# Float32r projections in layers 0, 2 and 3, weight magnitudes on ACT, and a moved residual and norm in a four-layer megakernel

## The reference, cut to what matters

```python
x = x + _L0_xattn_ref(_layernorm(x), ctx_1024, mask, ...)   # 16 heads of 16, softmax over 4096 keys
x = x + _L0_attn_ref(_layernorm(x), ...)
x = x + _L0_ffn_ref(_layernorm(x), L0_ffn_w1, ...)
x = x + _L1_xattn_ref(...); x = x + _L1_attn_ref(...); x = x + _L1_ffn_ref(...)   # 16 experts, top 2
x = x + _L2_xattn_ref(ctx_1024, _layernorm(x)); x = x + _L2_attn_ref(...); x = x + _L2_ffn_ref(...)
x = x + _L3_xattn_ref(_layernorm(x), ctx_1024, ctx_1024, ...); x = x + _L3_attn_ref(...)
x = x + _L3_ffn_ref(...)                                      # two layers inside
# layer 0, attention: h is the normed x with scale and bias
c_q = h @ w_down_q.T;  c_kv = h @ w_down_kv.T
q = c_q @ w_up_q.T;  k = c_kv @ w_up_k.T;  v = c_kv @ w_up_v.T    # 128 -> 1024 each, then rotary on q and k
# layer 0, feed-forward: weights are rounded to -1, 0, 1
scale = 1.0 / jnp.clip(jnp.mean(jnp.abs(w)), 1e-05)
wq = jnp.clip(jnp.round(w * scale), -1, 1) / scale
# layer 2, attention: t is the rms-normed x; q, k, v are 1024 wide, a gate per head
q = t @ Wq;  k, v = split(t @ Wkv)
# layer 2, feed-forward
out = sigmoid(xr @ W_r.T) * (square(relu(xk @ W_k.T)) @ W_v.T)
# layer 3, cross attention: of each head's 16 keys the top KEEP = 11 stay; linear attention
# layer 3, feed-forward, each of two layers: attention of 8 heads, then
a, g = split(layernorm(x) @ w1 + b1);  x = x + (a * gelu(g)) @ w2 + b2
```

## Time and profile before

| what | value |
|---|---|
| median of 3 runs | 2007.03 us (2000.08 to 2008.4) |
| the profiled execution's own time | 2001.91 us |
| its span | 2000.6 us |
| PE, DVE, ACT, POOL busy | 95%, 68%, 62%, 35% of the span |
| mean granted TensorE clock | 0.989 |
| instructions | 38492 |

### The profile page before, as it was taken

How to read it: one execution, slowest core, us unless ns; L and a number is a source line. 1 busy time by engine, 2 the same in 40 slices (tenths; PEclk the granted TensorE clock), 3 DMA queues, 4 the chain that set the end, 5 groups by cost and what they waited for, 6 DMA issues and landing times.

```text
span 2000.6 us, 38492 instructions
## 1 busy us (share of the span) xinstructions
PE 1894.7 (95%) x14304; PEld 1204.0 (60%) x14329; DVE 1354.4 (68%) x3178; ACT 1248.9 (62%) x2811; POOL 706.3 (35%) x899
## 2 busy tenths in 40 slices
PE   7999999989999899999999999999999899899999
PEld 4555665545465645566555556879657688565656
DVE  3677668765486677766879577774356998578382
ACT  3687778867363458777888673367265786265251
POOL 2123331173460211333110155676042566355151
PEclk9999999987999999999999999999999999999999
DMA  9677668753011497766876113164102342200110
GB/s 214 145 147 150 120 120 164 127 92 106 1 43 53 77 149 148 152 118 122 164 128 93 37 52 98 49 204 123 48 22 77 93 120 61 90 1 9 43 57 11
DMA packets 114362, 191.58 MB, mean 96 GB/s; under 512 B 17224, under 2 KB 67201, under 8 KB 107649
## 3 DMA queue, kind: packets, MB, share of 16 engines
q1 hardware_dynamic: 113184, 188.11, 42.9%
q10 hardware_dynamic: 992, 1.02, 0.2%
HBM read 135.20 MB, written 2.69 MB: 69 GB/s over the span
## 4 chain that ended last, share of the span: by engine, by line
PE 66%; DVE 21%; ACT 7%; issue 2%; POOL 2%; DMA 1%; SPq 0%; POOLq 0%; ACTq 0%; DVEq 0%
DVE WK L900 10%; PE PS L837 8%; PE PS L708 8%; PE PS L738 6%; PE PS L381 5%; PE PS L389 4%; PE PS L696 4%; ACT WK L586 3%; PE PS L2499 2%; PE PS L539 2%; PE PS L2441 2%; PE PS L491 2%; PE PS L518 2%; PE PS L754 2%; PE PS L1369 1%
## 5 line engine op out<-in xcount | busy, mean ns | idle before, releaser
L900 DVE TENSOR_REDUCE WK<-PS 128x1 f32<-128x1024 f32 x512 | 621.1, 1223 | 218.4 <-PE PS L708 170.3
L1008 ACT ACTIVATE WK<-PS 128x512 f32<-128x512 f32 x840 | 464.9, 601 | 45.0 <-PE PS L708 30.8
L708 PEld LDWEIGHTS PS<-QSR,KSR 51*128 51x128 f32 x2048 | 253.3, 189 | 242.0 <-ACT WK L1008 92.0
L708 PE MATMUL PS<-QSR,KSR 51*128 51x256 f32 x2048 | 381.4, 309 | 8.9 <-DVE WK L900 0.9
L696 PE MATMUL PS<-KSR,QSR 51*128 51x512 f32 x1024 | 371.6, 452 | 3.6 <-DMA KSR<-scratch_mask 2.8
L837 PE MATMUL PS<-WK 128*32 128x256 f32 x2528 | 223.4, 400 | 0.5 <-ACT WK L992 0.5
L614 POOL TENSOR_SCALAR WK<-WK 128x256 f32<-128x256 f32 (+1 forms) x320 | 150.9, 472 | 164.3 <-ACT WK L586 62.9
L1023 POOL TENSOR_TENSOR WK<-WK 128x512 fp32r<-128x512 f32 x62 | 79.2, 1278 | 350.9 <-ACT WK L969 177.0
L696 PEld LDWEIGHTS PS<-KSR,QSR 51*128 51x128 f32 x1024 | 187.2, 187 | 13.2 <-DVE WK L900 6.5
L586 ACT ACTIVATE WK<-PS,WK 128x256 f32<-128x256 f32 (+1 forms) x320 | 140.4, 450 | 62.3 <-DVE WK L558 42.0
L1126 POOL TENSOR_SCALAR nbw<-WK 128x4 fp32r<-128x4 f32 x64 | 12.6, 197 | 314.2 <-DVE WK L906 313.3
(11 more groups left out here) (388 smaller groups left out, 3897.9 us busy)
## 6 DMA issues: line engine op xcount, KB each, us to landing
KSR<-WK SPq DMA_DIRECT2D x381, 128.0 KB
WB<-in_ctxT SPq DMA_DIRECT2D x78, 512.0 KB, 5.1
WK<-in_ctxT SPq DMA_DIRECT2D x40, 512.0 KB, 4.1
WK<-in_ctx SPq DMA_DIRECT2D x32, 512.0 KB, 3.9
WA<-in_ctxT SPq DMA_DIRECT2D x26, 512.0 KB, 5.1
QSR<-scratch_q SPq DMA_DIRECT2D x48, 128.0 KB, 4.4
WB<-in_L3f_qkv SPq DMA_DIRECT2D x2, 1536.0 KB, 6.3
WB<-in_L3f_w SPq DMA_DIRECT2D x2, 1536.0 KB, 10.2
```

Source lines behind the costliest of these rows:

```text
L708: return pe.e.matmul(tile["S", L, s, i][:, j * 256:j * 256 + 256], KS[s % 4][HALF[i % 2], kt * 128:(kt + 1) * 128], QS[HALF[i % 2], g % 2, ...
L900: dv.e.tensor_reduce(mt[:, n:n + 1], tile["R", L, s, n].rearrange("p a b -> p (a b)"), AX, ALU.max).then_inc(*dv.at("R", L, s, n))
L1008: ac.e.activation(PR[n % NPR], tile["S", L, s, i], ACT.Exp).then_inc(*ac.at("E", L, s, i))
```

## The change

It has five parts.

1. *Cross attention 0.* POOL's `magnitude` and `total` go. ACT computes Abs of each half weight with a sum over its columns, after the Exp of score tiles 5 and 13 of step 26 and 5 and 9 of step 27 (`ABS`), and TensorE adds the halves. `last` is issued at the start of step 25. POOL splits the four up-projection weights into a high part in `CXR` and a low part in `WBR` (`split_up`) in its last three turns. One normalisation of the first head group (`normalise`) is done some row maxima later.
2. *Layer 0's attention.* The query and key tiles are three float32r matmuls each; `c0` is split by DVE and ACT.
3. *Layer 2's attention.* The first two query tiles stay float32; keys, values and the other six query tiles are float32r, in this order. High parts are made by ACT, low parts of weights by POOL, of activations by DVE.
4. *Layer 2's feed-forward and cross attention 3.* DVE's tail keeps its product; POOL adds the residual in one instruction, DVE takes the norm's statistics over units 4 to 7, ACT the inverse root by Ln and Exp, POOL normalises at 8, TensorE transposes at 9. Unit 0 moves from the sixth place to the eleventh. `fill` counts change.
5. *Layer 3's feed-forward.* Of each layer's twelve `w1` tiles, eight are float32r.

```diff
+        def feat_split_pe(name, wh, wl, c0, high, low, *freed):
+            b = take(banks, name, *freed)
+            settle(b)
+            m = slice(c0, c0 + 128)
+            for k in range(2):
+                pe.e.matmul(b.ap, wh[k][:, m], high[:, k, :], start=k == 0, stop=False)
+            for k in range(2):
+                pe.e.matmul(b.ap, wl[k][:, m], high[:, k, :], start=False, stop=False)
+            for k in range(2):
+                i = pe.e.matmul(b.ap, wh[k][:, m], low[:, k, :], start=False, stop=k == 1)
+            i.then_inc(*pe.at(*name))
+        ABS = ((26, 5), (26, 13), (27, 5), (27, 9))
...
                     if L == 0 and s == 28:
+                        pe.wait_ge(ac, "wabs", 3)
                         for i in range(2):
-                            pe.wait_ge(po, "wabs", i)
                             pe.e.matmul(b.ap[:, 1, 384 + i:385 + i], onesf[:, :], wst[:, 4 * i:4 * i + 1], start=True,
+                                        stop=False)
+                            pe.e.matmul(b.ap[:, 1, 384 + i:385 + i], onesf[:, :], wst[:, 4 * i + 3:4 * i + 4], start=False,
                                         stop=True).then_inc(*pe.at("wsum", i))
...
                     ac.e.activation(PR[n % NPR], tile["S", L, s, i], ACT.Exp).then_inc(*ac.at("E", L, s, i))
+                    if L == 0 and (s, i) in ABS:
+                        j = ABS.index((s, i))
+                        ac.wait_ge(pe, "F", L, 23, 7)
+                        ac.wait_ge(d_l0f)
+                        ac.wait_ge(ac)
+                        ac.e.activation(WK[:, 16384:17408], WA[:, 1024 * j:1024 * j + 1024], ACT.Abs,
+                                        accum_out=wst[:, j // 2 * 4 + j % 2 * 3:j // 2 * 4 + j % 2 * 3 + 1]).then_inc(
+                            *ac.at("wabs", j))
...
+        def split_up(j):
+            raw = WL0a[UP0[j]][:, 0, :]
+            po.wait_ge(d_l0a)
+            po.wait_ge(po)
+            po.e.tensor_scalar(UH0[j], raw, 1.0, 1.0, ALU.mult, ALU.mult).then_inc(*po.at())
+            po.wait_ge(po)
+            po.e.tensor_tensor(UL0[j], raw, UH0[j].bitcast(F), ALU.subtract).then_inc(*po.at("u0", j))
...
-                    if L == 0 and s == 25:
-                        magnitude(0, 0)
-                        magnitude(0, 1)
-                    if L == 0 and s == 26:
-                        total(0)
-                        magnitude(1, 0)
-                    if L == 0 and s == 27:
-                        magnitude(1, 1)
-                        total(1)
...
+                    if L == 0 and s > 28:
+                        po.wait_ge(pe, "F", L, 23, 7)
+                        for j in ((0,), (1,), (2, 3))[s - 29]:
+                            split_up(j)
...
-                elif o == ("S", 28, 0) and L == 0:
+                if o == ("S", 25, 0) and L == 0:
                     last()
...
                     for u in range(2):
-                        x = pe.e.matmul(b.ap[:, u, :], WL0a[n + ("", "s")[u]][:, 0, m * 128:(m + 1) * 128], CQ[:, i, :],
-                                        start=True, stop=True)
+                        j = 2 * i + u
+                        pe.e.matmul(b.ap[:, u, :], UH0[j][:, c], CQH[:, i, :], start=True, stop=False)
+                        pe.e.matmul(b.ap[:, u, :], UL0[j][:, c], CQH[:, i, :], start=False, stop=False)
+                        x = pe.e.matmul(b.ap[:, u, :], UH0[j][:, c], CQL[:, i, :], start=False, stop=True)
...
+            for m in range(2):
+                feat_pe(("q2", m), WL2a["q"], m * 128, HT, 2, (dv, "q2", m))
+            for f in range(2):
+                pe.wait_ge(ac, "h2a", "hi", f)
+                pe.wait_ge(dv, "h2a", "lo", f)
+                pe.wait_ge(po, "w2", "k", f)
             for m in range(8):
-                feat_pe(("q2", m), WL2a["q"], m * 128, HT, 2, (dv, "q2", m))
-                feat_pe(("k2", m), WL2a["kv"], m * 128, HT, 2, (ac, "k2", m))
+                feat_split_pe(("k2", m), KVH2, KVL2, m * 128, HHA, HLA, (ac, "k2", m))
...
+            po.wait_ge(dv, "rms2", NT - 1)
+            for k in range(2):
+                po.wait_ge(ac, "w2", "k", k)
+                po.e.tensor_tensor(KVL2[k][:, 0:1024], WL2a["kv"][:, k, 0:1024], KVH2[k][:, 0:1024].bitcast(F),
+                                   ALU.subtract).then_inc(*po.at("w2", "k", k))
...
                 dv.e.tensor_tensor(RR[:, t, :], tile["v2f", t][:, 0:256], RR[:, t, :], ALU.mult).then_inc(*dv.at("v2f", t))
-                dv.wait_ge(dv)
-                dv.e.tensor_tensor(X[:, t, :], X[:, t, :], RR[:, t, :], ALU.add).then_inc(*dv.at())
-                if t == NT - 1:
-                    end(dv, "l2f")
-                ln_a("ln3x", X, t)
-                if t:
-                    ln_b("ln3x", X, XN, t - 1)
-            ln_b("ln3x", X, XN, NT - 1)
+            end(dv, "l2f")
...
-        unit = [*range(1, 6), 0, *range(6, NU)]
+        unit = [*range(1, 11), 0, *range(11, NU)]
...
-            again = {2: 7, 3: 26, 10: 9, 17: 9}
+            again = {2: 7, 3: 9, 15: 9, 17: 9}
...
-                if u == 3:
-                    turn_pe("h3x", XN, (dv, "ln3x"), dv, ac, filled=(10, 4, 4, 0))
+                if u == 9:
+                    turn_pe("h3x", XN, (po, "ln3x"), dv, ac, ring=ring3)
...
+                if 4 <= u < 8:
+                    dv.wait_ge(po, "x2f")
+                    ln_a("ln3x", X, u - 4)
...
+                if u == 3:
+                    po.wait_ge(dv, "v2f", NT - 1)
+                    po.e.tensor_tensor(X[:, :, :], X[:, :, :], RR, ALU.add).then_inc(*po.at("x2f"))
...
+            for m in range(2, 6):
+                gated_pe(("fa", l, m), l, m, 0, (dv, "ag", l, m))
+                gated_pe(("fg", l, m), l, m, 1, (ac, "gg", l, m))
```

187 lines of the change are left out of this document (139 added, 48 removed).

## The result

The changed kernel takes 1974.96 us at the median of four runs (1969.93 to 1978.51), the kernel before 2007.72 us (2000.08 to 2009.35): a ratio of 0.9842, 95% interval 0.9807 to 0.9878. It is faster by 32.8 us, or 1.6%, instead of the 46.5 us worked out, and 2 us above the range. The profiled execution took 1978.51 us, the longest of its four; that of the kernel before took 2001.91 us, 5.8 us under its median. So the two traces differ by less than the medians do, and what follows from their rows is one pair of executions.

A forecast was written before the change was run, and what follows sets the result against it. TensorE was taken as the bound, with waits and half-clock matmuls in cross attention 0. Terms -20.3 - 18.6 - 7.6 = -46.5 gave 1955.4 from the profile, 1960.5 from the median; predicted 1958, range 1949 to 1967, widened by rivals to 1945 to 1973.

The forecast's parts named there:

- Part 1: Cross attention 0's tail: magnitudes move from POOL to ACT; -23.8 us for POOL's work removed, +3.5 for Abs, -20.3.
- Part 2: Cross attention 0: layer 0's weights load before step 25 instead of after all keys; key rows keep 3 us margin, cost 0.
- TensorE waiting for `KSR` rows: Cross attention 0: sign that the prediction is wrong, TensorE standing idle for key rows.
- a clock of 0.5 after step 26: Cross attention 0: sign that the prediction is wrong, a granted clock of 0.5 following step 26.
- Rival (d): Cross attention 0: key rows of steps 29 to 31 land late behind the weights, 2030 us; chance 0.02, milder 0.01.
- Everything but (d) is faster by over 2%: Whole kernel: every outcome except late key rows was to beat the kernel before by over 2%.
- rival (a): Cross attention 0, steps 26 to 28: the clock falls again, costing 8 or 16 us, 1966 to 1974; chance 0.17.
- Part 3: Layers 0, 2 and 3: float32 calls become three float32r matmuls, -5.6 - 7.4 - 5.6 = -18.6 us.
- The contention that I had put into the range: Layers 2 and 3: DVE's subtractions wait beside POOL's, +2 us in all, put into the range only.
- Part 4: Cross attention 3's ramp: selection transposes of the third unit 9.8 us earlier, partly given back, -7.6 us; bounds -9.8 and -3.
- +1.1, +0.6 and +0.5: Cross attention 3, us given back: eight transposes in a TensorE-bound stretch, ACT's copy of `HT`, DVE's added work.
- rival (b): Cross attention 3: ramp gives little, DVE bounds the first ten units, subtractions wait for POOL, +6 to +7, 1965; chance 0.14.

The follow-up runs named there:

- The fewer bytes at the same place: Changed kernel with only an eighth of the columns of the six large weight transfers loaded, output wrong: 1966.74 us, ratio 0.9817.
- the three groups: Changed kernel with the twelve weight transfers cut into three groups, at the starts of steps 25, 26 and 27: 1963.70 us, ratio 0.9800.
- the two later places: Changed kernel with the twelve weight transfers in one piece at the start of step 26 (1966.83 us) or step 27 (1967.20 us) instead of 25.
- the later place: Changed kernel with the transposes of the normed x and unit 0 one place later in cross attention 3: 1967.99 us, ratio 0.9825.
- the run in which the clock stayed at 1.00 there: Changed kernel with 13 instead of 9 dummy matmuls ahead of the second unit's transposes and 9 more ahead of the third's: 1976.74 us, ratio 0.9862.
- the ramp undone: Changed kernel with residual and norm back in DVE's tail, unit 0 at the sixth place, dummy matmuls as before: 1976.37 us, ratio 0.9868.

## Why the prediction was wrong

**Part 1 (-20.3) was right.** Alone it gave -20.6 in the tail (and -16.1, with an interval of 10.8 to 22.6, between the medians). The Abs were 1.25 us instead of 1.35, and the steps grew by about as much as reckoned (91.5 us against the 88.3 of cross attention 1: +3.2, where +3.5 was taken).

**Part 2 (0) was the step that failed.** It put the early load at no cost, and the load cost 7 to 8 us at the median and 16.1 us in the profile. "TensorE waiting for `KSR` rows" and a clock of 0.5 after step 26, two of the prediction's own signs of being wrong, both came. The prediction gave the key rows of step 29 a margin of 3 us: issued by 428, "landed by about 431", needed at 434. The issue came at 430.8 and the need at 435.6, both near. The landing came at 442.4. I had taken each transfer's time when it moves nearly alone ("the weights moved at full rate when alone") and chained them by their issue. But the queue's issue runs ahead of its bytes: when SP had issued the last weights, at 423, the windows show 5 more us at 370 to 410 GB/s, about 2 MB, and the key rows, at 125 to 139 GB/s with a DMA share above 1.0, need 6 us of all engines a step. A sum over the engines would have shown that there was no margin: from 406.9 on, one step of key rows (6 us), 4.25 MB of weights (11 us) and two more steps of key rows (12 us) are, by this estimate, 29 us of full engines, which end at 436 at best; it gives the sign and not the 442.4. The fewer bytes at the same place (91.5 us), the three groups and the two later places with all bytes (91.5 us each) show that the early load in one piece is the cause; that the bytes count for more than the issuing follows from the 3.8 us at most that the issue moved; how much the key rows of step 30 add, no run separates. The Trainium skill, "DMA: Bandwidth & Descriptors", section "Issuing engines are not separate DMA queues", says that all transfers share the same 16 DMA engines and interleave, whoever starts them; by that too the margin has to be reckoned over the engines and not over a list. The trace agrees: the engines' share stays at 1.03 to 1.14 while weights and the rows of two steps move. Rival (d) named this mechanism, with the point from which it decides, 3 us, and gave it 0.03. Its price was too high, 72 us, because I let it strike three steps; it struck one, and cost 5 to 16 us in the four profiles with the wait. "Everything but (d) is faster by over 2%" did not agree with the prediction's own rival (a), whose 1966 to 1974 lies almost wholly above the 1966.9 that 2% would need; the change is faster by 1.6%.

**The price of a wait is its own length and the clock behind it.** 6.95 us of waiting came with 24 us at 1.2 GHz and cost 16.1 us of tail; 7.85 us came with the rest of the tail at 1.2 GHz and cost 21.5; 5.04, 3.75 and 2.17 us cost 10.4, 5.3 and 6.9.

**Part 3 (-18.6) was right**: -5.46, -7.08 and -5.55, 18.1 together. A call of three matmuls is 0.68 us. The contention that I had put into the range is there: beside POOL's subtractions DVE's two of 512 columns took 1.98 us each. TensorE waited 0.43 us for them behind its four float32 calls. These are POOL's, DVE's and PE's rows of it in the timelines:

```profile
1413.04 5.12 POOL L2354 TENSOR_TENSOR WBR<-WB,CXR 128x1024 fp32r<-128x1024 f32 x2 [14.47 <-DVE WK L2130]
```

```profile
1414.76 3.95 DVE L2306 TENSOR_TENSOR CXR<-HT,CXR 128x512 fp32r<-128x512 f32 x2
```

```profile
1418.97 0.70 PE L399 MATMUL PS<-CXR 128*128 128x512 f32 x2 [0.43 <-DVE CXR L2306]
```

**Part 4 (-7.6) had its gain right and its cost wrong.** The transposes of the third unit came 9.9 us nearer (-9.8). Of the give-back I had +1.1, +0.6 and +0.5. The first two are 2.1 us when the norm is ready, as the later place shows. They were 6.9 because I never asked when POOL would have written the normed x: it stands behind a subtraction and a product of two units, ends after 1599.07, and the transposes were due at 1595.2. With a clock of 0.88 over the unit this made the rest. "+0.5" for DVE was +1.5, by the run in which the clock stayed at 1.00 there: its busy time over five units rose from 39.08 to 42.99 us, of which the four pairs of statistics (0.61 each) are 2.4; the rest was not traced. Over the five units together DVE has no time to spare, as rival (b) had it; unit by unit it and TensorE are level. Its 1965 lacked part 2.

**The sum.** With the measured terms, -20.6 - 18.1 - 1.9 = -40.6, and +16.1 for the wait makes -24.5; the spans differ by 23.4. Without the wait -40.6 is what the three groups show: 1963.7 against 2003.3, -39.6. Between the medians the change misses the forecast of -46.5 by 13.7 us; the 7 to 8 us of the early load and the 5.7 of part 4 account for it. The missing part 4 alone would have left the time in the range; part 2 took it out.

## What to carry to other kernels

When a bulk load is moved ahead of small, timed transfers, add up the work of all DMA engines from then to the deadline; issue times alone do not tell, and inefficient small rows count by their share of engines, not by their bytes. Cut the bulk into pieces that fit what each step leaves free, or start it later; both took the wait away here. When work is moved onto an engine that is far from full (POOL here, twice), find its place in that engine's list and the end of what stands ahead of it, before taking its cost as zero. And a stretch at 1.2 GHz cost next to nothing where DVE had as much to do (43.29 us against 43.10 and 43.00), while in the tail, where TensorE does, it cost 1.5 to 13.7 us on top of the wait.

## What was not expected of the hardware

The key rows' landing varied from one execution to the next with the same instructions up to there: 12.4, 11.3, 9.1, 8.5 and about 6 us behind the last issue, and TensorE's wait for them was 6.95, 5.04, 3.75, 2.17 and none. And a wait's length did not tell the length of the lower clock: 3.75 us stood ahead of 6 us of work at 1.2 GHz, 2.17 us ahead of 14, and gaps of 0.3 and 0.4 us ahead of 10. In cross attention 3 a wait of 3.77 us left the clock at 1.00 in the trace of before, and the same wait with the ramp undone was followed by a granted clock of 0.96 over five units.
